# Column sums of the messages in the first pass: VectorE adds four tiles, TensorE gets one matmul a group

## What is computed

```python
h = relu(layernorm(x))                          # 12500 x 128
m = concat([h[src], 0, edge_attr]) @ W1 + b1    # 212500 x 256
m = relu((m - mean(m, 0)) * rsqrt(var(m, 0) + EPS) * g1 + be1)
agg = segment_mean(m, dst)                      # 12500 x 256
h2 = concat([h, 0, agg]) @ W2 + b2              # 12500 x 385, batch norm and relu again
out = x + relu(relu(bn(h2)) @ W3 + b3)
```

## Time and profile before

| what | value |
|---|---|
| median of 3 runs | 3194.51 us (3186.86 to 3200.58) |
| the profiled execution | 3181.97 us |
| its span, first to last instruction | 3180.2 us |
| TensorE busy / clock granted | 77% of the span / 0.856 of 2.4 GHz |
| VectorE, ScalarE, GpSimd busy | 44%, 30%, 55% |
| DMA | 740.85 MB, 233 GB/s in the mean |

### The profile page before, as it was taken

The page is one execution under the profiler, slowest core; times in us unless marked ns, Lnnn a source line. Parts: engine busy times, 40 slices in busy tenths (PEclk is TensorE's granted clock), DMA queues, the critical chain, the costliest instruction groups (busy, mean ns, idle before and its releaser), DMA issues. The chain is left out here.

```text
span 3180.2 us, 34295 instructions
## 1 busy us (share of the span) xinstructions
PE 2441.9 (77%) x12138; PEld 914.3 (29%) x12138; DVE 1393.9 (44%) x2299; ACT 969.7 (30%) x1601; POOL 1749.7 (55%) x1850
## 2 busy tenths in 40 slices
PE   4666767657767777777777677777867999999998
PEld 3412112112212222222222122222213433444448
DVE  4422212234323333322333233333223899999878
ACT  3322212112212221222122122212213655655546
POOL 6466666666666666666666666666664222222220
PEclk8888778778878888888888888888876999999999
DMA  8466656666656666666666566566664999999965
GB/s 237 155 210 215 212 194 224 209 221 239 216 194 227 212 213 207 218 204 207 216 229 208 190 223 218 195 228 220 212 206 150 337 350 350 345 343 345 341 238 162
DMA packets 270622, 740.85 MB, mean 233 GB/s; under 512 B 46391, under 2 KB 98661, under 8 KB 270448
## 3 DMA queue, kind: packets, MB, share of 16 engines
q1 hardware_dynamic: 189152, 525.28, 46.2%
q0 software_dynamic: 78432, 212.46, 22.4%
q10 hardware_dynamic: 2864, 0.86, 0.1%
HBM read 501.63 MB, written 236.81 MB: 232 GB/s over the span
## 5 line engine op out<-in xcount | busy, mean ns | idle before, releaser
L621 POOL DMA_INDIRECT sums<-P_d,late x1581 | 1496.5, 947 | 796.4 <-issue 453.3
L1052 DVE TENSOR_TENSOR sums<-psum,sums 128x1024 f32<-128x1024 f32 x396 | 479.0, 1220 | 1524.2 <-remote 823.9
L1351 PE MATMUL psum<-late,sums 128*128 128x512 f32 x1660 | 950.3, 687 | 255.2 <-issue 168.4
L709 ACT ACTIVATE sums<-sums 128x1024 f32<-128x1024 f32 x416 | 437.7, 1054 | 1720.7 <-remote 988.0
L1294 PE MATMUL psum<-sums,ones 128*32 128x512 f32 x830 | 486.5, 667 | 117.8 <-issue 70.2
L1351 PEld LDWEIGHTS psum<-late,sums 128*128 128x128 f32 x1660 | 315.4, 210 | 888.6 <-issue 728.0
L1297 PE MATMUL psum<-sums,ones 128*32 128x512 f32 x830 | 497.9, 676 | 59.5 <-issue 58.6
L1296 PE MATMUL psum<-sums,ones 128*32 128x512 f32 x830 | 494.5, 676 | 36.5 <-issue 35.9
L1295 PE MATMUL psum<-sums,ones 128*32 128x512 f32 x830 | 488.7, 670 | 28.8 <-issue 28.6
L1095 DVE TENSOR_TENSOR late<-late,psum 128x1024 f32<-128x1024 f32 (+1 forms) x407 | 482.6, 1212 | 34.3 <-DMA late<-m_d 32.5
L650 POOL TENSOR_TENSOR late<-dst_f,iota 128x384 f32<-128x384 f32 (+1 forms) x139 | 115.1, 829 | 379.4 <-PE psum L1463 375.3
(11 more groups left out here) (215 smaller groups left out, 2012.0 us busy)
## 6 DMA issues: line engine op xcount, KB each, us to landing
m_d<-sums SPq DMA_DIRECT2D x415, 512.0 KB
late<-m_d SPq DMA_DIRECT2D x406, 512.0 KB, 5.5
sums<-in_ea_main SPq DMA_DIRECT2D x103, 512.0 KB
sums<-P_d,late POOLq DMA_INDIRECT x1581
P_d<-sums SPq DMA_DIRECT2D x24, 512.0 KB
nodes<-in_x SPq DMA_DIRECT2D x24, 256.0 KB
late<-in_x SPq DMA_DIRECT2D x24, 256.0 KB, 3.1
out<-late SPq DMA_DIRECT2D x24, 256.0 KB, 2.4
```

The source lines that it names most:

```text
L621: pool.indirect_dma_start(out=m_s[s][0:r, k * L:(k + 1) * L], out_offset=None, in_=P1_d, in_offset=bass.IndirectOffsetOnAxis(ap=idx[0:r, G ...
L709: act.activation(q_s[g % Q_SLOTS][0:r, 0:w], m_s[g % M_SLOTS][0:r, 0:w], ACT.Square).then_inc(s_q, 1)
L1052: dve.tensor_tensor(m_s[s][0:r, 0:w], ps_m[place_m[g]][0:r, 0:w], m_s[s][0:r, 0:w], ALU.add).then_inc(s_m, 1)
L1351: ins = pe.matmul(ps_m[place_m[g]][:, 2 * i * L:2 * (i + 1) * L], ea[:, i * P:(i + 1) * P], W1c[:, :], start=True, stop=g not in xg_no, sk ...
```

## The change

VectorE gets the four-tile sums. Per group it runs two reductions over the tiles, one of m (128 x 1024 to 128 x 256) and one of the squares, into a slot `sum_s` of 512 columns. It does those of group g - 1 after the add of group g. `stats(g)` is then one matmul of 512 columns with 32 columns of ones, and it runs four steps behind instead of three. What waited for `s_st` (ScalarE, GpSimd, and VectorE in the computed groups) now waits for `s_sums`, sent by the second reduction; VectorE itself waits for `s_st` of two groups earlier before it writes a `sum_s` slot again. The squares have two slots instead of three; the two sum slots fill the space of the third. The last group of 20 edges is summed as before. After the pass the totals need one copy instead of a copy and an add, and four small matmuls instead of two.

```diff
-Q_SLOTS = 3
+Q_SLOTS = 2
+SUM_SLOTS = 2
+SUM_LAG = 4
...
                 if g >= M_SLOTS:
                     pool.wait_ge(s_mw[s], 16 * (g // M_SLOTS))
-                    pool.wait_ge(s_st, g - M_SLOTS + 1)
+                    pool.wait_ge(s_sums, g - M_SLOTS + 1)
...
                 if g >= Q_SLOTS:
-                    act.wait_ge(s_st, g - Q_SLOTS + 1)
+                    act.wait_ge(s_sums, g - Q_SLOTS + 1)
...
+            def tile_sums(g):
+
+                out = sum_s[g % SUM_SLOTS]
+                if g >= SUM_SLOTS:
+                    dve.wait_ge(s_st, g - SUM_SLOTS + 1)
+                dve.wait_ge(s_m, g + 1)
+                dve.tensor_reduce(out[:, 0:L], m_s[g % M_SLOTS].rearrange("p (t f) -> p f t", f=L), AX.X, ALU.add)
+                dve.wait_ge(s_q, g + 1)
+                dve.tensor_reduce(out[:, L:], q_s[g % Q_SLOTS].rearrange("p (t f) -> p f t", f=L), AX.X, ALU.add).then_inc(s_sums, 1)
...
                 if g in ranges:
                     ranges[g]()
+                if g >= 1:
+                    tile_sums(g - 1)
                 if g in count_at:
                     count_rows(count_at[g])
...
             dve.wait_ge(s_st, NG)
-            dve.tensor_copy(totals, ps_tot[:, 0:L]).then_inc(s_half, 1)
-            dve.wait_ge(s_half, 1)
-            dve.tensor_tensor(totals, totals, ps_tot[:, L:], ALU.add).then_inc(s_tot, 1)
+            dve.tensor_copy(totals, ps_tot[0:SPAN, :]).then_inc(s_tot, 1)
...
             def stats(g):
 
-                pe.wait_ge(s_q, g + 1)
...
                 if g < GF:
-                    pe.matmul(ps_tot[0:32, :], ones[:, 0:32], m[:, 0:2 * L], start=(g == 0), stop=False, skip_group_check=True)
-                    pe.matmul(ps_tot[32:64, :], ones[:, 0:32], m[:, 2 * L:], start=(g == 0), stop=(g == last), skip_group_check=True)
-                    pe.matmul(ps_tot[64:96, :], ones[:, 0:32], q[:, 0:2 * L], start=(g == 0), stop=False, skip_group_check=True)
-                    ins = pe.matmul(ps_tot[96:128, :], ones[:, 0:32], q[:, 2 * L:], start=(g == 0), stop=(g == last), skip_group_check=True)
+                    pe.wait_ge(s_sums, g + 1)
+                    ins = pe.matmul(ps_tot[0:SPAN, :], ones[:, 0:SPAN], sum_s[g % SUM_SLOTS], start=(g == 0), stop=(g == GF - 1),
+                                    skip_group_check=True)
...
-                if g >= 3:
-                    stats(g - 3)
+                if g >= SUM_LAG:
+                    stats(g - SUM_LAG)
```

More of the change, by code:

```diff
@@ L151, in n1_rows @@
             return sums[:, 0, c0 - BN_:c0 - BN_ + n] if b else spare[:, 0:n]
-        taken = [1024 * (M_SLOTS + Q_SLOTS + EA_SLOTS)]
+        taken = [1024 * (M_SLOTS + Q_SLOTS + EA_SLOTS) + 2 * L * SUM_SLOTS]
         def early(cols, parts=P):
@@ L163, in build @@
         ea_s = [flat[:, 1024 * (M_SLOTS + Q_SLOTS + i):1024 * (M_SLOTS + Q_SLOTS + i + 1)] for i in range(EA_SLOTS)]
+        sum_at = 1024 * (M_SLOTS + Q_SLOTS + EA_SLOTS)
+        sum_s = [flat[:, sum_at + 2 * L * i:sum_at + 2 * L * (i + 1)] for i in range(SUM_SLOTS)]
         assert M_SLOTS >= ROW_SLOTS + 2 and ROW_SLOTS * BN_ <= 2048
@@ L220, in build @@
         fb_hot_lo = late[:, 3 * EW + GE // 2:3 * EW + GE].bitcast(BF16).rearrange("p (k n) -> p k n", k=GT)
-        totals = mid[:, 0:L]
+        totals = mid[0:SPAN, 0:2 * L]
         diag = mid[:, 2 * L:3 * L].rearrange("p (h f) -> p h f", h=2)
@@ L307, in build @@
         t_col = sb("t_col", [P, 2])
-        pick = sb("pick", [P, 2])
+        pick = sb("pick", [SPAN, 1])
         g1_col, be1_col = sb("g1_col", [P, 2]), sb("be1_col", [P, 2])
@@ L366, in build @@
         s_st = sem("s_st")
-        s_pick, s_half, s_tot, s_fin = sem("s_pick"), sem("s_half"), sem("s_tot"), sem("s_fin")
+        s_pick, s_sums, s_tot, s_fin = sem("s_pick"), sem("s_sums"), sem("s_tot"), sem("s_fin")
         s_eat = sem("s_eat")
@@ L608, in _ @@
             pool.wait_ge(s_pick, 1)
-            for i in range(4):
-                pool.memset(pick[32 * i:32 * i + 1, i // 2:i // 2 + 1], 1.0 / E).then_inc(s_pick, 1)
+            pool.memset(pick[0:1, :], 1.0 / E).then_inc(s_pick, 1)
             pool.wait_ge(s_ei, 48)
@@ L633, in _ @@
             flag = pool.alloc_register("wide_pool")
-            pool.wait_ge(s_pick, 5)
+            pool.wait_ge(s_pick, 2)
             pool.wait_ge(s_m, NG)
@@ L1046, in _ @@
                         dve.wait_ge(s_mw[s], 16 * (g // M_SLOTS))
-                        dve.wait_ge(s_st, g - M_SLOTS + 1)
+                        dve.wait_ge(s_sums, g - M_SLOTS + 1)
                     dve.tensor_tensor(m_s[s].rearrange("p (t f) -> p t f", f=L), ps_m[place_m[g]].rearrange("p (t f) -> p t f", f=L),
@@ L1288, in stats @@
             def stats(g):
-                pe.wait_ge(s_q, g + 1)
-                r, m, q = rows(g), m_s[g % M_SLOTS], q_s[g % Q_SLOTS]
-                last = GF - 1
                 if g < GF:
-                    pe.matmul(ps_tot[0:32, :], ones[:, 0:32], m[:, 0:2 * L], start=(g == 0), stop=False, skip_group_check=True)
-                    pe.matmul(ps_tot[32:64, :], ones[:, 0:32], m[:, 2 * L:], start=(g == 0), stop=(g == last), skip_group_check=True)
-                    pe.matmul(ps_tot[64:96, :], ones[:, 0:32], q[:, 0:2 * L], start=(g == 0), stop=False, skip_group_check=True)
-                    ins = pe.matmul(ps_tot[96:128, :], ones[:, 0:32], q[:, 2 * L:], start=(g == 0), stop=(g == last), skip_group_check=True)
-                else:
-                    pe.matmul(ps_tot[0:32, 0:L], ones[0:r, 0:32], m[0:r, 0:L], start=False, stop=True, skip_group_check=True)
-                    ins = pe.matmul(ps_tot[64:96, 0:L], ones[0:r, 0:32], q[0:r, 0:L], start=False, stop=True, skip_group_check=True)
+                    pe.wait_ge(s_sums, g + 1)
+                    ins = pe.matmul(ps_tot[0:SPAN, :], ones[:, 0:SPAN], sum_s[g % SUM_SLOTS], start=(g == 0), stop=(g == GF - 1),
+                                    skip_group_check=True)
+                else:
+                    r, m, q = rows(g), m_s[g % M_SLOTS], q_s[g % Q_SLOTS]
+                    pe.wait_ge(s_q, g + 1)
+                    pe.matmul(ps_tot[0:SPAN, 0:L], ones[0:r, 0:SPAN], m[0:r, 0:L], start=False, stop=True, skip_group_check=True)
+                    ins = pe.matmul(ps_tot[0:SPAN, L:], ones[0:r, 0:SPAN], q[0:r, 0:L], start=False, stop=True, skip_group_check=True)
                 ins.then_inc(s_st, 1)
@@ L1368, in _ @@
                     pe.transpose(psum[0:2 * GC, 7, 0:P], rng[:, :], ident[:, :]).then_inc(s_rngT, 1)
-            stats(NG - 3)
-            stats(NG - 2)
-            stats(NG - 1)
+            for g in range(NG - SUM_LAG, NG):
+                stats(g)
             pe.wait_ge(s_tot, 1)
-            pe.wait_ge(s_pick, 5)
+            pe.wait_ge(s_pick, 2)
             pe.wait_ge(s_m, NG)
             for h in range(2):
-                ins = pe.matmul(ps_fin[:, h, :], totals[:, h * P:(h + 1) * P], pick[:, :], start=True, stop=True)
+                for v in range(2):
+                    ins = pe.matmul(ps_fin[:, h, v:v + 1], totals[:, v * L + h * P:v * L + (h + 1) * P], pick[:, :],
+                                    start=True, stop=True)
             ins.then_inc(s_fin, 1)
```

## The result

The changed kernel takes 3451.89 us (3440.47 to 3456.83, 4 runs), the kernel before 3192.39 us (3186.86 to 3200.58, 4 runs). The ratio is 1.081, 95% interval 1.0784 to 1.0836. It is slower; the forecast was 3083 us, and its range ended at 3385.

The account below looks back on a forecast made before the run. GpSimd's gathers (1976 us) plus holds were taken to bound the first pass. With 41 holds it falls 113 us to 2168; 3181.97 - 113 + 2 = 3071, plus 12.5 for the runs' median, gives 3083 us, range 2910 to 3385.

Parts of the forecast that it names:

- Gather floor of 1976 us: First pass: 1581 indirect DMAs on GpSimd at 1.25 us each need 1976 us; the pass took 2281.3 us.
- holds: Stretches beside the gathers where several engines wait for late signals, read as TensorE's, until GpSimd pauses; some 70 reckoned.
- its rival without holds: First pass: fewer TensorE instructions make holds vanish and gathers bound, 2892 us; holds nearly gone (2892 to 2990) had chance 0.19.
- Four matmuls cost what one costs: TensorE's `stats`: four matmuls overlap and take 1.06 us, as one does; the change buys about 0.01 us a group.
- A reduction takes 1.2 us: VectorE, first pass: each new reduction of 1024 elements takes 1200 ns, two a group, 996 us in all.
- the case: Rival, VectorE's reductions: strided ones cost twice, 996 us more, pass 2750 us and up, time 3670; chance 0.03.
- the formula: First pass = max(1976, 1758 + 10 n) us for n holds, 1758 being VectorE's work and waits.
- Waits for `s_st` are 85 us and covered: VectorE waits at most 1.2 us in each of 71 count steps, 85 us, within 218 us of cover under the gathers.
- Holds come with the number of TensorE's instructions, n = 70 x 0.58 = 41: First pass: instructions fall from 11800 to 6820, holds from 70 to 41, pass 2168 us; chance 0.38.
- A hold takes 10 us of VectorE's time: First pass: of 14 us idle a hold, VectorE fills about 4 us with one step's reductions, leaving 10.
- Holds end when gathers end, in every example: Argument for the rival that gathers alone make holds, n stays 70: pass 2458 us, time 3374; chance 0.27.
- The clock: TensorE's clock, mean 0.82, would stay not under 0.75; the half-clock rival, about 3350 us, had chance 0.05.

Follow-up runs that it names:

- the kernel with neighbouring elements: Changed kernel, both reductions adding four neighbouring elements, so wrong sums: 2852.27 us beside 2844.84 without holds, 3340.87 beside 3207.19 with holds.
- one contiguous add: Kernel before, VectorE adding m's contiguous halves, squares' second half left out, stats two 512-column matmuls: 2902.1 us beside 2844.4 without holds, 3243.64 beside 3207.65 with.
- squares interleaved, four sum slots: Changed kernel with four sum slots, ScalarE writing a column's four squares as neighbours: 2862.36 us beside 2844.4 without holds, 3402.46 beside 3207.65 with.

## Why the prediction was wrong, point by point

- **Gather floor of 1976 us**: right. Without holds the gathers of the kernel before start from 110.9 to 2088.3 us, 1977 us (2845 in all, slots' pauses 14 us), and half the gathers take 667 us out. But the forecast had no price for the 35 us that holds cost ahead of the pass: its rival without holds came to 2892, and the kernel with neighbouring elements takes 2852.
- **Four matmuls cost what one costs**: right where there are no holds, 0.9994 and 0.9998 without the other three. With holds it is 0.9937.
- **A reduction takes 1.2 us**: the step that failed first. 1.92 and 1.88. The rows were of neighbouring elements, and the text took the same price for elements 1 KB apart, with twice that as the other bound. The truth lay between, and the case had a chance of 0.03 only. (Its 3670 us also left out the holds, which the formula adds: with 41 of them the pass would be 1758 + 996 + 410 = 3164 us, not 2750.) VectorE's work in the pass became 2162 us instead of 1673, above the gathers' 1976, and with it everything hung on VectorE. Over 1.5 us a reduction was the prediction's own first sign of being wrong.
- **Waits for `s_st` are 85 us and covered**: the size was right (93.0 us with neighbouring elements), the cover was not. 132.1 us before L1050 in the changed kernel without holds, and 151 us of its time.
- **Holds come with the number of TensorE's instructions, n = 70 x 0.58 = 41**: the step that failed second, and it alone turns the sign: at the reckoned price the kernel is 4.1% slower with holds, not 3.5% faster. With 0.58 of the instructions the pauses stay (311 of 325 us). Counted in the timelines from 200 us on, GpSimd pauses over 3 us 67 times in the kernel before, 54 times with one matmul and 73 times with neighbouring elements; at 0.58 of the instructions the forecast had 41. With n = 70 kept and the reckoned price of 1.2 us, the prediction's own formula gives 2458 us for the pass, and 2439 was measured, with two errors in the sum that nearly cancel (1593 us of work for 1673, 847 us of waits for 785).
- **A hold takes 10 us of VectorE's time**: right in total while VectorE has cover (847 us of idle time in the run with neighbouring elements, 700 + 85 reckoned); number and length apart weren't measured. Not in the changed kernel: 677 + 1576 + 85 + 700 would be 3038 us, and the pass takes 2554. Its "remote" waits are fewer, as the row below shows; my reading is that a VectorE that is always late makes GpSimd pause anyway, and TensorE's signals catch up in those pauses. That wasn't tested.

```profile
DVE sums L1050 <- remote: 233.9, 45, 12.0
```

- **"Holds end when gathers end, in every example"**: true of the three examples, not of the trace. Of the add's 113 waits for "remote" in the first pass of the kernel before, 45 end where the gather before and the one after both follow at the usual gap, 299 of 824 us, as here:

```profile
911.80 0.94 POOL L621 DMA_INDIRECT sums<-P_d,late  x1 [0.30 <-issue]
913.00 1.23 DVE L1052 TENSOR_TENSOR sums<-psum,sums 128x1024 f32<-128x1024 f32 x1 [9.17 <-remote]
913.05 0.95 POOL L621 DMA_INDIRECT sums<-P_d,late  x1 [0.30 <-issue]
```

- **The clock**: right, 0.82 in the first pass of both kernels.
- **Sign**: two mechanisms, each slower. With holds, the arrangement at the reckoned price costs 4.1%, and the distance of the reductions about as much again (1.081). Without holds the arrangement costs 0.3%, and the distance, with the wait that it uncovers, all the rest of 12.3%.

What the holds cost each kernel, put together from series with and without them (medians, us):

| Kernel | without | with | difference |
|---|---|---|---|
| before | 2844 | 3207 | 363 |
| one matmul of four | 2846 | 3185 | 339 |
| one contiguous add | 2902 | 3244 | 342 |
| changed | 3193 | 3452 | 259 |
| changed, neighbouring elements | 2853 | 3341 | 488 |
| squares interleaved, four sum slots | 2862 | 3402 | 540 |

Work put on VectorE under the cover of the gathers is free without holds and is paid for with them: the two last kernels have 0.9 ms (1592 against 677 us) and 1.3 ms (415 x 3.17 us) more of it in the pass than the one before, and lose most. (The changed kernel with holds stood beside 3192, the others beside 3207.) The changed kernel has most work on VectorE and loses least; the point above on the price of a hold has a reading of that, not a test. What makes the holds, and why a series has them or not, is open. The chip alone doesn't decide it: the one numbered 0 in the record had holds in one series and none in another, where each kernel ran once. The traces show that holds don't follow TensorE's instructions. That it is TensorE's signals that come late is a reading too, since the profile can't name the sender, and no run took the gathers away where there were holds.

No version here that computes all the sums is faster than the kernel before.

## What to carry to other kernels

Before the price of a known instruction is used for a new one, compare how both step through memory: with its float32 elements 16 bytes or more apart a reduction cost 1.9 us where it cost 1.2 with neighbours, and that alone turned an engine with 218 us of cover into the bound. Cover is to be reckoned for the worst case in which the kernel is run: the same added work cost 0.3% without holds and 4.1% with them. And a mechanism guessed from two stretches of a trace (here: stalls in proportion to instructions) deserves the chance of a guess until one run has varied its cause.

## What the runs showed of the hardware

- One step in the price of a reduction, between a distance of 8 bytes (1.207 us) and 16 bytes (1.965 us), and none from there to 1 KB (1.916), for VectorE's reduction of 128 x 1024 to 128 x 256 float32. ScalarE pays likewise for a write at 16 bytes: 2.08 us instead of 1.06.
- A gather issued by GpSimd while VectorE adds two operands in SBUF takes 1.19 us in the mean and up to 1.47 instead of 0.95. It cost 4% of the kernel where VectorE itself had time to spare.
- The kernel before runs in 2844 us in some series and in 3207 in others, the latter with holds: waits of 7 us in the mean (810 us in 111) for signals whose sender the profile doesn't name. All runs of one series behave alike.
